# Phase 1 of a metaformer block: x also loaded by channels and scaled there, scatters in two groups of four, xr normalised in two halves

## The chip, the cores and the metric

One core of one Trainium2 chip. The metric is device time in microseconds (us); the kernel before takes 1960.43 us, the median of 3 runs (1958.6 to 1961.08).

## What is computed

The input x is (16, 56, 56, 96) in fp32, 50176 tokens of 96 channels. First a "conv" block: x is normalised over its channels, cut into windows of 7 x 7 and normalised once more (both together are one centring and one scale per token, with a small rescaling of the variance), and a linear recurrence runs over the 49 tokens of each window. Its output `xr` is normalised again and goes through an MLP 96 to 384 to 96. Then a mixture of experts, two of four per token.

```python
w = _ln(_ln_c(x) cut in 7x7 windows, ln1_w, ln1_b)
xs = w @ Bm                          # 49 steps per window
h = xs[t] + h @ A                    # the recurrence
xr = h @ Cm
y = gelu(_ln(xr, ln2_w, ln2_b) @ W1 + b1) @ W2 + b2
x = x + xr + y
t = _ln_t(x); probs = softmax(t @ gate_w + gate_b), two largest kept and rescaled
x = x + sum_e masked[e] * (gelu(t @ w1[e] + b1[e]) @ w2[e] + b2[e])
```

## The kernel before

The work has two phases. Phase 1 runs over 49 tiles; tile t holds the t-th token of all 1024 windows, so that the recurrence goes from tile to tile. A tile is 8 groups of 128 tokens (`SUBS`), tokens on partitions, or 96 channels on partitions by 1024 tokens after a transpose. Each token's row (its sum, its gate scores, its normalised value, its number) is scattered to DRAM, sorted by the pair of experts that it chose. Phase 2 reads the sorted rows in 103 blocks of 512 tokens and runs the experts; the change does not touch it.

The order in phase 1 is written out by hand: every engine has its own loop `for p in periods()`, and semaphores tie the engines. In period p TensorE (PE) does, in this order: the recurrence for tile r = p+1 (`from_state(r)`, L1067, which adds A times the state, then `from_input(r)`, L1074, which adds B times `x_t`) into `mix_ps`; two `up` products of tile p (L1039 to L1041); the rank products of tile p-2 (L1095); `sum_xr(r)` (L1080), which overwrites `mix_ps` with xr by tokens; `down` and `up` in turn (L1048); eight transposes of the normalised x of tile p+2 (L1026, `x_n` to `turn_ps`); `turn_y(p, 0)` (L1056); `down(p, 4)`, `down(p, 5)`; eight transposes of the normalised xr (L1026, `xr_n` to `turn_ps`); `turn_y(p, 1)`. `mix_ps` has one buffer: `from_state(r+1)` waits until xr of tile r has been normalised.

ScalarE (ACT) in period p: `y_hi` from `turn_ps` (L565); four of the eight `normalise_x(p+2)` (L522); `h_t` from `mix_ps` (L572); GELU 0 and 1 (L548); the other four of `normalise_x`; four of `normalise_rows(p-2)` (L539); GELU 2 and 3; `copy_y(p, 0)` (L557); GELU 4; `normalise_xr(r)`, eight instructions (L532); GELU 5; `x_t` from `turn_ps` (L593); `copy_y(p, 1)`.

VectorE (DVE) in period p: `y_lo` (L834); `add_x2(p-1, 1)` (L769); statistics of the sum of tile p-1, of x of tile p+3 and of xr of tile r (L712, L718, L723); `take_xr(r)` (L730 to L736); `shift_of_r` (L742), which waits for GpSimd; `positions(p-2)` (L818 to L828); `add_x2(p, 0)`, which waits for `turn_y(p, 0)`; `shift_of_x(p+3)` (L748, L750); `shift_of_rows`, `gate(p-1)` (L776 to L808); four of `normalise_rows(p-1)` (L760).

GpSimd (POOL) in period p: the inverse deviation of xr (`rstd_of_r`, L423), those of x and of the sum in one instruction (L436), then the eight scatters of tile p-2 (L447). Both are powers of a variance that DVE has written. SyncE (SP) loads x, up to five tiles ahead (L297). The lines on which the change rests:

```python
                if tile(p + 2):                                  # PE
                    turn.take(pe, x_t_ok, p + 3)
                    pe.wait_ge(x_n_ok, p + 3)
                    to_channels(x_n[:, (p + 2) % 2, :, :]).then_inc(x_turned, 1)
...
                if tile(p + 2):                                  # ACT
                    act.wait_ge(x_turned, p + 3)
                    if p + 2 >= 1:
                        act.wait_ge(h_summed, p + 2)
                    act.copy(x_t[0:C, :], turn_ps[0:C, :]).then_inc(x_t_ok, 1)
```

Of the kernel before, what the change touches and what calls it, by code (L numbers as in the profile page):

```python
# [57 lines left out]
X_RING = 5  # L58
DEV_RING = 4
# [17 lines left out]
X_FIRST = 2  # L77
# [8 lines left out]
def periods():  # L86
    return range(-3, TILES + 2)
# [14 lines left out]
def build_program(nc, x, up_w, state_w, turned_w, mlp_down_w, down_w, gate_w, up_b, gate_b, down_b, ln_wb, out):  # L102
# [16 lines left out]
    with ctx:
# [43 lines left out]
        x_n = sb("x_n", [P, 2, SUBS, C])  # L163
# [16 lines left out]
        shift_x = sb("shift_x", [P, 2, SUBS])  # L180
        shift_t = sb("shift_t", [P, HALF_SUBS])
# [111 lines left out]
        def _(sp):  # L293
# [89 lines left out]
        def _(pool):  # L383
# [41 lines left out]
            def rstd_of_x_and_t(t):  # L425
# [6 lines left out]
                if 2 <= t < TILES + 2:  # L432
                    pool.wait_ge(x_n_ok, t - 1)
# [803 lines left out]
```

## Time and profile before

| | us |
|---|---|
| median of 3 runs | 1960.43 |
| the profiled execution | 1960.39 |
| its span, first to last instruction | 1958.7 |
| PE busy over the span | 1871.8 (96%) |
| ACT busy | 1599.1 (82%) |
| DVE busy | 1490.5 (76%) |
| POOL busy | 1355.4 (69%) |

Phase 1 takes the first 950 us or so, 49 tiles at 17.77 us each in its steady part, and phase 2 the rest. Busy matmul time is modelled, since matmuls overlap, so the distance between the starts of PE's rows says more than its busy share: 17.77 us is such a distance, from the first `from_state` row of one period to that of the next.

### The profile page before, as it was taken

The page shows a single profiled execution, that of the slowest core. Times are in us where ns is not written, and L with a number is a line of the kernel's source. Part 1 is how long each engine was busy: PE and PEld are TensorE (multiplying, and loading weights), DVE is VectorE, ACT ScalarE, POOL GpSimd, SP SyncE. Part 2 cuts the span into 40 slices and gives each one's busy share as a digit, 9 for nine tenths or more (in the row PEclk, how much of TensorE's full clock was granted, in tenths as well). Part 3 has the DMA queues.
Part 4 walks back from the last instruction along what each step waited for, and adds up shares of the span by engine and source line. Part 5 has one row for each costly group of instructions (what it writes and reads, how often), then busy time and mean ns, then how long its engine had stood idle before and what let it go on. Part 6 is the DMA issues. An engine that isn't in the chain of part 4 may idle for free.

```text
span 1958.7 us, 36640 instructions
## 1 busy us (share of the span) xinstructions
PE 1871.8 (96%) x8883; PEld 1302.6 (67%) x8883; DVE 1490.5 (76%) x6676; ACT 1599.1 (82%) x3068; POOL 1355.4 (69%) x1097
## 2 busy tenths in 40 slices
PE   5979999999999999997599999999999999999996
PEld 3546666666666666664377777777777777777774
DVE  5767887788777877786477777777777777777775
ACT  3868887888888888875499989999999899999995
POOL 3357767776767677667477777777777777777775
PEclk9989999999999999998699999999999999999998
DMA  4042212222222222111666666666666666666662
GB/s 127 28 114 68 71 67 69 68 71 67 71 67 71 67 70 69 61 51 52 214 211 211 208 207 204 206 206 209 213 208 209 206 202 206 214 210 212 209 208 75
DMA packets 121158, 272.93 MB, mean 139 GB/s; under 512 B 26148, under 2 KB 34749, under 8 KB 120946
## 3 DMA queue, kind: packets, MB, share of 16 engines
q1 hardware_dynamic: 85840, 209.93, 35.6%
q0 software_dynamic: 32000, 58.87, 8.7%
q10 hardware_dynamic: 3106, 1.78, 0.3%
q8 instruction: 74, 1.21, 0.3%
q14 instruction: 138, 1.13, 0.2%
HBM read 204.47 MB, written 66.98 MB: 139 GB/s over the span
## 4 chain that ended last, share of the span: by engine, by line
PE 50%; POOL 27%; issue 20%; DVE 1%; DMA 1%; POOLq 0%; ACTq 0%; ACT 0%; SPq 0%; DVEq 0%
POOL sorted_rows L447 19%; PE mix_ps L1170 7%; PE mix_ps L1171 7%; PE mix_ps L1172 7%; POOL rstd_xt L436 7%; PE turn_ps L1156 4%; PE up_ps L1156 4%; PE turn_ps L1157 4%; PE turn_ps L1158 4%; PE up_ps L1157 4%; PE up_ps L1158 4%; PE tok_ps L1179 3%; PE y_ps L1142 2%; POOL rows L444 1%; POOL rstd_r L423 0%
## 5 line engine op out<-in xcount | busy, mean ns | idle before, releaser
L480 POOL DMA_INDIRECT out<-out_sb,idx x412 | 424.1, 1029 | 262.7 <-DVE out_sb L968 156.2
L924 DVE TENSOR_TENSOR g_lo<-g,g_hi 128x512 fp32r<-128x512 f32 x618 | 423.9, 686 | 198.5 <-ACT g_hi L613 198.5
L447 POOL DMA_INDIRECT sorted_rows<-rows,pos x392 | 383.3, 978 | 118.9 <-issue 104.8
L613 ACT CAST g_hi<-g 128x512 fp32r<-128x512 f32 x618 | 380.8, 616 | 13.1
L1048 PE MATMUL y_ps<-g,d_mlp 128*100 128x512 f32 x588 | 307.2, 604 | 6.5 <-ACT g L548 1.8
L469 POOL TENSOR_TENSOR ex<-euler,rows 128x16 f32<-128x16 f32 x103 | 305.2, 2963 | 10.1 <-DMA rows<-sorted_rows 9.7
L1170 PE MATMUL mix_ps<-g_hi,ew 128*96 128x512 f32 x618 | 244.1, 395 | 0.2 <-DVE g_lo L924 0.2
L1171 PE MATMUL mix_ps<-g_hi,ew 128*96 128x512 f32 x618 | 244.0, 395 | 0.0
L1172 PE MATMUL mix_ps<-g_lo,ew 128*96 128x512 f32 x618 | 243.7, 394 | 0.0
L548 ACT ACTIVATE g<-up_ps 128x512 f32<-128x512 f32 x294 | 172.7, 605 | 60.1 <-PE up_ps L1041 54.9
L423 POOL TENSOR_TENSOR rstd_r<-var_eps,neg_half 128x8 f32<-128x8 f32 x49 | 81.7, 1668 | 193.0 <-DVE var_eps L723 193.0
L607 ACT ACTIVATE g<-turn_ps 128x512 f32<-128x512 f32 x310 | 184.4, 595 | 33.0 <-PE turn_ps L1158 19.4
L607 ACT ACTIVATE g<-up_ps 128x512 f32<-128x512 f32 x308 | 183.4, 595 | 29.4 <-PE up_ps L1158 16.7
L1039 PE MATMUL up_ps<-y_hi,w_hi 98*128 98x512 f32 x294 | 195.0, 663 | 1.8 <-DVE y_lo L834 1.8
L625 ACT ACTIVATE y_sb<-mix_ps,ew 96x512 f32<-96x512 f32 x206 | 140.9, 684 | 23.1 <-PE mix_ps L1172 2.0
L522 ACT ACTIVATE x_n<-x_in,shift_x,rstd_xt 128x96 f32<-128x96 f32 x392 | 150.3, 456 | 8.0 <-DVE shift_x L748 8.0
L436 POOL TENSOR_TENSOR rstd_xt<-var_eps,neg_half 128x16 f32<-128x16 f32 (+1 forms) x53 | 143.5, 2708 | 5.6 <-DVE var_eps L723 5.6
L532 ACT ACTIVATE xr_n<-mix_ps,shift_r,rstd_r 128x96 f32<-128x96 f32 x392 | 131.2, 447 | 17.9 <-DVE shift_r L742 17.8
L1156 PE MATMUL turn_ps<-y_hi,ew 98*128 98x512 f32 x310 | 136.4, 440 | 1.4 <-DVE y_lo L929 1.4
L1156 PE MATMUL up_ps<-y_hi,ew 98*128 98x512 f32 x308 | 134.7, 437 | 0.0
L769 DVE TENSOR_TENSOR rows<-tok_ps,x_xr 128x400 f32<-128x400 f32 x98 | 55.6, 567 | 103.2 <-PE tok_ps L1056 103.2
L1048 PEld LDWEIGHTS y_ps<-g,d_mlp 128*100 128x100 f32 x588 | 86.8, 167 | 65.0 <-ACT g L548 48.2
(181 smaller groups left out, 4164.9 us busy)
## 6 DMA issues: line engine op xcount, KB each, us to landing
ew<-expert_w SPq DMA_DIRECT2D x206, 384.0 KB, 4.2
ew<-expert_w SPq DMA_DIRECT2D x206, 288.5 KB, 3.5
rows<-sorted_rows SPq DMA_DIRECT2D x103, 394.0 KB
x_in<-in_x SPq DMA_DIRECT2D x49, 384.0 KB, 3.1
out<-out_sb,idx POOLq DMA_INDIRECT x412
sorted_rows<-rows,pos POOLq DMA_INDIRECT x392, 2.5
sorted_rows<-pad_rows SPq DMA_DIRECT2D x11, 394.0 KB, 5.0
expert_w<-w_hi SPq DMA_DIRECT2D x4, 192.0 KB, 3.9
```

Of the source, the lines that this page charges most:

```text
L436: pool.tensor_tensor(rstd_xt[:, t % 2, which, :], var_eps[:, 1 + which.start:1 + which.stop, :], neg_half[:, which, :], ALU.pow).then_inc( ...
L447: pool.indirect_dma_start(out=sorted_rows[:, :], out_offset=bass.IndirectOffsetOnAxis(ap=pos[:, r, s:s + 1], axis=0), in_=rows[:, r, s, :] ...
L469: pool.tensor_tensor(ex[:, b % 2, :, :], euler[:, :].rearrange("p (s e) -> p s e", s=BSUBS), rows2[:, b % IN_RING, :, COL_BELOW:COL_T], AL ...
L480: pool.indirect_dma_start(out=out_rows, out_offset=bass.IndirectOffsetOnAxis(ap=idx[:, r, s:s + 1], axis=0), in_=out_sb[:, r, s, :], in_of ...
L607: act.activation(g[:, n % G_RING, :], up_bank(n), ACT.Gelu).then_inc(gelu2_done, 1)
L613: act.copy(g_hi[:, n % PART_RING, :], g[:, n % G_RING, :]).then_inc(hi_done, 1)
L924: dve.tensor_tensor(g_lo[:, n % PART_RING, :], g[:, n % G_RING, :], f(g_hi[:, n % PART_RING, :]), ALU.subtract).then_inc(lo_done, 1)
L1048: pe.matmul(y_ps[0:CG, :], d_mlp[:, k, :], g[:, n % G_RING, :], start=(k == 0), stop=(k == KB - 1)).then_inc(down_done, 1)
L1156: pe.matmul(up_bank(n), hi[0:KR, :], t_hi, start=True, stop=False)
L1170: pe.matmul(y2_bank(q), hi, g_hi[:, part, :], start=(k == 0), stop=False)
L1171: pe.matmul(y2_bank(q), lo, g_hi[:, part, :], start=False, stop=False)
L1172: pe.matmul(y2_bank(q), hi, g_lo[:, part, :], start=False, stop=(k == KB - 1)).then_inc(down2_done, 1)
```

## The change

x is loaded twice: by tokens as before (it still serves the statistics and the residual), and by channels, 96 partitions by 1024 tokens, into `x_raw_t` with two buffers (`load_x_t`). The inverse deviations of x are written to DRAM as a row (`rstd_rows`, 128 partitions by 32 bytes) and read back to 96 partitions, 4 KB to each (`turn_rstd`). DVE multiplies the two (`scale_x`); the row of deviations lies with the 8 groups of one partition side by side, so it is read with a step of 8 elements. The centring goes into the weights (`b_aug`, once). With that the eight `normalise_x`, the eight transposes of x and the copy of `x_t` are gone. All eight `normalise_rows` run on ACT. The second half of a tile's scatters comes one period later, ahead of `rstd_of_r`, behind a wait on `h_summed`. `normalise_xr` is two groups of four with GELU 4 and 5 between them, and the transposes of xr wait for each half. `turn_y(p, 1)` moves behind `from_state` of the next period.

```diff
+            def load_x_t(t):
+                if t >= XT_RING:
+                    sp.wait_ge(x_t_ok, t - XT_RING + 1)
+                sp.dma_start(x_raw_t[:, t % XT_RING, :], x_chan[t, :, :]).then_inc(x_t_loaded[t % XT_RING], 16)
+
+            def turn_rstd(t):
+
+                sp.wait_ge(rstd_xt_ok, t + 1)
+                sp.dma_start(rstd_rows[t, :].rearrange("(p s) -> p s", s=SUBS), rstd_xt[:, t % 2, 0, :]).then_inc(rstd_saved, 16)
+                if t >= 1:
+                    sp.wait_ge(x_t_ok, t)
+                sp.wait_ge(rstd_saved, 16 * (t + 1))
+                sp.dma_start(rstd_t[:, :], rstd_rows[t:t + 1, :].to_broadcast([C, TOK])).then_inc(rstd_t_loaded, 16)
...
+            for t in range(XT_RING, TILES):
+                load_x_t(t)
+                if t + X_RING - XT_RING < TILES:
+                    load_x(t + X_RING - XT_RING)
+                turn_rstd(t)
+                if t == X_RING + 1:
+                    save_experts()
...
                 if 2 <= t < TILES + 2:
-                    pool.wait_ge(x_n_ok, t - 1)
+                    pool.wait_ge(rstd_saved, 16 * (t - 1))
...
             for p in periods():
+                if tile(p - 3):
+                    if tile(p + 1):
+
+                        pool.wait_ge(h_summed, p + 2)
+                    scatter(p - 3, range(HALF_SUBS, SUBS))
                 if tile(p + 1):
                     rstd_of_r(p + 1)
                 if tile(p + 3) or tile(p - 1):
                     rstd_of_x_and_t(p + 3)
                 if tile(p - 2):
-                    scatter(p - 2, range(SUBS))
+                    scatter(p - 2, range(HALF_SUBS))
...
+            def normalise_xr(t, part):
                 if part == 0:
-                    act.wait_ge(shift_x_ok, t + 1)
-                    if t >= 2:
-                        act.wait_ge(x_turned, t - 1)
+                    act.wait_ge(shift_r_ok, t + 1)
+                    if t >= 1:
+                        act.wait_ge(xr_turned, t)
                 for s in range(part * HALF_SUBS, (part + 1) * HALF_SUBS):
...
-                ins.then_inc(xr_n_ok, 1)
+                ins.then_inc(xr_n_ok if part == 1 else xr_half_ok, 1)
...
+            def scale_x(t):
+                i = t % XT_RING
+                dve.wait_ge(x_t_loaded[i], 16 * (t // XT_RING + 1))
+                dve.wait_ge(rstd_t_loaded, 16 * (t + 1))
+                if t >= 1:
+                    dve.wait_ge(h_summed, t)
+                dve.tensor_tensor(x_t[0:C, :].rearrange("c (s p) -> c s p", s=SUBS), x_raw_t[:, i, :].rearrange("c (s p) -> c s p", s=SUBS),
+                                  rstd_t[:, :].rearrange("c (p s) -> c s p", s=SUBS), ALU.mult).then_inc(x_t_ok, 1)
...
                 if tile(p - 2):
                     positions(p - 2)
+                if tile(p + 2):
+                    scale_x(p + 2)
                 if tile(p):
                     add_x2(p, 0)
...
                 if tile(p - 1):
                     shift_of_rows(p - 1)
                     gate(p - 1)
-                    normalise_rows(p - 1)
...
                 if tile(r):
                     from_state(r)
+                if tile(p - 1):
+                    turn_y(p - 1, 1)
+                if tile(r):
                     from_input(r)
...
-                if tile(p + 2):
-                    turn.take(pe, x_t_ok, p + 3)
-                    pe.wait_ge(x_n_ok, p + 3)
-                    to_channels(x_n[:, (p + 2) % 2, :, :]).then_inc(x_turned, 1)
...
                 if tile(r):
                     turn.take(pe, y_lo_ok, r + 1)
+                    pe.wait_ge(xr_half_ok, r + 1)
+                    to_channels(xr_n, 0)
                     pe.wait_ge(xr_n_ok, r + 1)
-                    to_channels(xr_n).then_inc(xr_turned, 1)
-                if tile(p):
-                    turn_y(p, 1)
+                    to_channels(xr_n, 1).then_inc(xr_turned, 1)
```

On PE, from the last `down` ahead of the transposes to the first `up` of the next period, the order was this (a row ends with the semaphores on which it waits):

```order
L1048 MATMUL y_ps<-g,d_mlp 100x512 [waits y_copied,gelu_done]
L1026 MATMUL turn_ps<-ident,x_n 96x128 [waits x_n_ok,y_lo_ok]
L1026 MATMUL turn_ps<-ident,x_n 96x128 x7
L1056 MATMUL tok_ps<-ident,y_sb 128x100 [waits y_copied,base_set]
L1048 MATMUL y_ps<-g,d_mlp 100x512 [waits gelu_done] x2
L1026 MATMUL turn_ps<-ident,xr_n 96x128 [waits xr_n_ok,x_t_ok]
L1026 MATMUL turn_ps<-ident,xr_n 96x128 x7
L1056 MATMUL tok_ps<-ident,y_sb 128x100 [waits y_copied,x2_ok]
L1067 MATMUL mix_ps<-h_t,a_aug 100x512 [waits xr_n_ok,x_xr_ok,h_t_ok]
L1074 MATMUL mix_ps<-x_t,b_aug 100x512 [waits x_t_ok]
```

and is now this:

```order
L1069 MATMUL y_ps<-g,d_mlp 100x512 [waits y_copied,gelu_done]
L1077 MATMUL tok_ps<-ident,y_sb 128x100 [waits y_copied,base_set]
L1069 MATMUL y_ps<-g,d_mlp 100x512 [waits gelu_done] x2
L1047 MATMUL turn_ps<-ident,xr_n 96x128 [waits xr_half_ok,y_lo_ok]
L1047 MATMUL turn_ps<-ident,xr_n 96x128 x3
L1047 MATMUL turn_ps<-ident,xr_n 96x128 [waits xr_n_ok]
L1088 MATMUL mix_ps<-h_t,a_aug 100x512 [waits xr_n_ok,x_xr_ok,h_t_ok]
L1077 MATMUL tok_ps<-ident,y_sb 128x100 [waits y_copied,x2_ok]
L1095 MATMUL mix_ps<-x_t,b_aug 100x512 [waits x_t_ok]
```

The eight transposes of `x_n` are gone, those of `xr_n` have two waits and no longer wait for the copy of `x_t`, and the second `tok_ps` group stands behind `from_state` (L1088).

On DVE the middle of a period, between `positions` and `gate`, read

```order
L828 CAST pos<-place_sum 128x8
L769 TENSOR_TENSOR rows<-tok_ps,x_xr 128x4x100
L748 SCALAR_TENSOR_TENSOR shift_x<-moment,rstd_xt 128x8
L750 TENSOR_TENSOR dev_x<-var_eps,rstd_xt 128x8
L755 SCALAR_TENSOR_TENSOR shift_t<-moment,rstd_xt 128x4
```

and reads

```order
L846 CAST pos<-place_sum 128x8
L778 TENSOR_TENSOR x_t<-x_raw_t,rstd_t 96x1024
L787 TENSOR_TENSOR rows<-tok_ps,x_xr 128x4x100
L764 TENSOR_TENSOR dev_x<-var_eps,rstd_xt 128x8
L769 SCALAR_TENSOR_TENSOR shift_t<-moment,rstd_xt 128x8
```

`scale_x` (L778) stands ahead of `add_x2(p, 0)`, `shift_x` is gone. On POOL one period is now

```order
L475 DMA sorted_rows<-rows,pos 306688x197 [waits h_summed]
L475 DMA sorted_rows<-rows,pos 306688x197 x3
L451 TENSOR_TENSOR rstd_r<-var_eps,neg_half 128x8 [waits xr_n_ok,var_ok0]
L464 TENSOR_TENSOR rstd_xt<-var_eps,neg_half 128x16 [waits rstd_saved,t_n_ok,var_ok2,var_ok1]
L472 TENSOR_SCALAR rows<-ids 128x8 [waits t_n_ok,pos_step]
L475 DMA sorted_rows<-rows,pos 306688x197 [waits id_ok]
L475 DMA sorted_rows<-rows,pos 306688x197 x3
```

where eight scatters in one run stood behind L444 before.

## Rows read from the trace of the kernel before

**Rows 1.** Busy by stretch: PE, PEld, DVE, ACT, POOL; PEclk, DMA share, GB/s

```profile
300.00:500.00 200.00, 198.71 (x900) 122.70 (x900) 162.16 (x980) 162.44 (x349) 141.36 (x126) 1.00 0.21 69
...
950.00:1958.00 1008.00, 986.55 (x4944) 755.58 (x4944) 767.90 (x2369) 888.65 (x1545) 729.09 (x515) 0.99 0.66 202
```

**Rows 2.** Timeline of PE, one period: start, us, operation, count

```profile
409.07 1.88 PE L1067 MATMUL mix_ps<-h_t,a_aug 96*100 96x512 f32 x4
410.79 1.88 PE L1074 MATMUL mix_ps<-x_t,b_aug 97*100 97x512 f32 x4
...
422.15 1.03 PE L1026 MATMUL turn_ps<-ident,x_n 128*96 128x128 f32 x8
423.02 0.51 PE L1056 MATMUL tok_ps<-ident,y_sb 100*128 100x100 f32 x4
...
425.44 1.04 PE L1026 MATMUL turn_ps<-ident,xr_n 128*96 128x128 f32 x8
426.47 0.54 PE L1056 MATMUL tok_ps<-ident,y_sb 100*128 100x100 f32 x4
426.84 1.45 PE L1067 MATMUL mix_ps<-h_t,a_aug 96*100 96x512 f32 x3
```

**Rows 3.** Timeline of PE's weight loads: idle before, releaser

```profile
424.50 0.25 PEld L1048 LDWEIGHTS y_ps<-g,d_mlp 128*100 128x100 f32 x2 [0.96 <-ACT g L548]
425.36 0.86 PEld L1026 LDWEIGHTS turn_ps<-ident,xr_n 128*96 128x96 f32 x8 [0.61 <-ACT x_t L593]
```

**Rows 4.** Timeline of ACT, the same period

```profile
421.28 2.67 ACT L532 ACTIVATE xr_n<-mix_ps,shift_r,rstd_r 128x96 f32<-128x96 f32 x8
423.80 0.64 ACT L548 ACTIVATE g<-up_ps 128x512 f32<-128x512 f32 x1
```

**Rows 5.** Timeline of DVE, the same period

```profile
420.20 0.19 DVE L742 SCALAR_TENSOR_TENSOR shift_r<-moment,rstd_r 128x8 f32<-128x8 f32 x1 [0.74 <-POOL rstd_r L423]
...
423.57 0.58 DVE L769 TENSOR_TENSOR rows<-tok_ps,x_xr 128x400 f32<-128x400 f32 x1 [2.07 <-PE tok_ps L1056]
...
426.77 1.02 DVE L760 TENSOR_SCALAR rows<-rows,moment,rstd_xt 128x96 f32<-128x96 f32 x4
427.71 1.21 DVE L834 TENSOR_TENSOR y_lo<-turn_ps,y_hi 96x1024 fp32r<-96x1024 f32 x1
```

**Rows 6.** Groups of DVE by form, 100 to 850 us: busy us, mean ns

```profile
L794 DVE TENSOR_REDUCE rank<-beaten 128x32 f32<-128x128 f32 x41 | 11.7, 286 | 1.4
...
L826 DVE TENSOR_REDUCE place_sum<-place 128x8 f32<-128x48 f32 x42 | 10.2, 243 | 1.5
L801 DVE TENSOR_TENSOR of_pair<-kept 128x24 f32<-128x24 f32 x41 | 8.9, 218 | 1.4
```

**Rows 7.** Timeline of POOL, the same period

```profile
418.49 1.67 POOL L423 TENSOR_TENSOR rstd_r<-var_eps,neg_half 128x8 f32<-128x8 f32 x1 [2.83 <-DVE var_eps L723]
420.15 2.89 POOL L436 TENSOR_TENSOR rstd_xt<-var_eps,neg_half 128x16 f32<-128x16 f32 x1
...
425.00 0.96 POOL L447 DMA_INDIRECT sorted_rows<-rows,pos  x1 [0.30 <-issue]
```

**Rows 8.** Timeline of DVE while POOL's L436 runs

```profile
420.81 0.21 DVE L824 TENSOR_TENSOR place<-place,of_pair 128x48 f32<-128x48 f32 x1
421.05 0.24 DVE L826 TENSOR_REDUCE place_sum<-place 128x8 f32<-128x48 f32 x1
```

**Rows 9.** DMA issues, 100 to 850 us: KB each, median us to landing

```profile
x_in<-in_x SPq DMA_DIRECT2D x43, 384.0 KB, 3.1
sorted_rows<-rows,pos POOLq DMA_INDIRECT x332, 2.5
```

**Rows 10.** Timeline of POOL: the first and the last of 49 L423, the last L436

```profile
32.14 1.64 POOL L423 TENSOR_TENSOR rstd_r<-var_eps,neg_half 128x8 f32<-128x8 f32 x1 [14.53 <-DVE var_eps L723]
...
898.11 1.67 POOL L423 TENSOR_TENSOR rstd_r<-var_eps,neg_half 128x8 f32<-128x8 f32 x1 [3.97 <-DVE var_eps L723]
...
925.44 1.67 POOL L436 TENSOR_TENSOR rstd_xt<-var_eps,neg_half 128x8 f32<-128x8 f32 x1 [1.25 <-DVE var_eps L723]
```

More of the change, by code:

```diff
@@ L58 @@
 X_RING = 5
+XT_RING = 2
 DEV_RING = 4
@@ L76 @@
 FIRST_LOADS, GATE_LOADS, MLP_LOADS, LATER_LOADS = 4, 4, 3, 2
-X_FIRST = 2
 GATE_SUMS = 4
@@ L86, in periods @@
 def periods():
-    return range(-3, TILES + 2)
+    return range(-3, TILES + 3)
 class Region:
@@ L162, in build_program @@
         x_in = sb("x_in", [P, X_RING, SUBS, C])
-        x_n = sb("x_n", [P, 2, SUBS, C])
+        x_raw_t = sb("x_raw_t", [C, XT_RING, TOK])
+        rstd_t = sb("rstd_t", [C, TOK])
         x_t = sb("x_t", [C + 1, TOK])
@@ L231, in build_program @@
         x_loaded = [sem(f"x_loaded{i}") for i in range(X_RING)]
+        x_t_loaded = [sem(f"x_t_loaded{i}") for i in range(XT_RING)]
+        rstd_saved, rstd_t_loaded = sem("rstd_saved"), sem("rstd_t_loaded")
         const_step = sem("const_step")
@@ L307, in _ @@
             sp.dma_start(f(w_hi[C + 1:KR, 0:HID]), f(b_lo[:, 0:HID])).then_inc(bias_rows, 16)
-            for t in range(X_FIRST, X_RING):
+            for t in range(XT_RING, X_RING):
                 load_x(t)
+            turn_rstd(1)
             sp.wait_ge(const_step, CONSTS)
@@ L575, in _ @@
                     gelu(p, 1)
-                if tile(p + 2):
-                    normalise_x(p + 2, 1)
                 if tile(p - 2):
@@ L583, in _ @@
                     copy_y(p, 0)
+                if tile(r):
+                    normalise_xr(r, 0)
+                if tile(p):
                     gelu(p, 4)
+                    gelu(p, 5)
                 if tile(r):
-                    normalise_xr(r)
-                if tile(p):
-                    gelu(p, 5)
-                if tile(p + 2):
-                    act.wait_ge(x_turned, p + 3)
-                    if p + 2 >= 1:
-                        act.wait_ge(h_summed, p + 2)
-                    act.copy(x_t[0:C, :], turn_ps[0:C, :]).then_inc(x_t_ok, 1)
+                    normalise_xr(r, 1)
                 if tile(p):
@@ L1022, in gate_products, with to_channels @@
                           start=True, stop=True).then_inc(gate_sums, 1)
-            def to_channels(src):
-                for s in range(SUBS):
+            def to_channels(src, h):
+                for s in range(HALF_SUBS * h, HALF_SUBS * (h + 1)):
                     ins = pe.transpose(turn_ps[0:C, sub(s)], src[:, s, :], ident[:, :])
@@ L1086, in _ @@
                     from_state(r)
+                if tile(p - 1):
+                    turn_y(p - 1, 1)
+                if tile(r):
                     from_input(r)
```

92 lines of the change are left out of this document (39 added, 53 removed).

## The prediction

> **What bounds the kernel now.** I read the busy times by stretch first. Between 300 and 500 us PE is busy for 198.7 of 200 us, DVE and ACT for 162, POOL for 141, at the full clock; the 1008 us behind 950 us are phase 2, which the change leaves alone [rows 1]. So only the length of a period in phase 1 can move, and a little at its two ends. The timeline of PE gives that length: from `from_state` at 409.07 to the next at 426.84 us, 17.77 us [rows 2]. Then the waits inside it. Eight transposes of x_n take 423.02 - 422.15 = 0.87 us. From the start of `turn_y` at 423.02 to the transposes of xr at 425.44 us lie 2.42 us, which hold four half-products of 0.43 us (four of the same kind take 410.79 - 409.07 = 1.72 us) and `turn_y`, 0.35 us: 0.35 us is left over [rows 2]. It is the wait for GELU 5 [rows 3], which ACT can start only at 423.80 us, behind eight `normalise_xr` from 421.28 us on [rows 4]. The transposes of xr take 426.47 - 425.44 = 1.03 us, 0.16 more than those of x_n [rows 2], since they wait for the copy of `x_t` [rows 3]. PE therefore loses 0.5 us of a period to ACT and is otherwise the bound.
>
> The other engines have room. In 17.77 us DVE stands idle for 0.74 us ahead of `shift_r` (it waits for the power on POOL) and 2.07 us ahead of `add_x2(p, 0)` (it waits for `turn_y`) [rows 5]. POOL stands idle for 2.83 us ahead of L423 [rows 7].
>
> **The change, part by part.**
>
> *PE.* Eight transposes go: -0.87. The waits for GELU 5 and for `x_t` go: -0.5. `turn_y(p, 1)` only moves, by 0.35 us to the other side of `from_state`: 0. In ACT's new order GELU 4 stands behind four `normalise_xr` instead of behind none. These last half of 2.67 us [rows 4], and PE arrives at `down(p, 4)` 0.87 us sooner; laid out from `from_state`, PE is there at 13.8 us and GELU 4 is done at 13.95 us: about +0.2. PE's own period would be 17.77 - 0.87 - 0.5 + 0.2 = 16.6 us. The two waits in place of one ahead of the transposes of xr cost nothing: the first half has been normalised 2 us before PE arrives, the second half at about the moment when the first four transposes end.
>
> *ACT.* It loses eight `normalise_x` and the 96x1024 copy, and gains four `normalise_rows`. It had room before; cost nothing.
>
> *DVE.* This is the crux. Taken out: the four `normalise_rows`, 427.71 - 426.77 = 0.94 us, and `shift_x`, 0.07 us. Put in: `scale_x`, ahead of `add_x2(p, 0)`, in the 2.07 us for which DVE stood idle there [rows 5]. If it fills them, the period of DVE is 17.77 - 2.07 - 0.94 - 0.07 + s = 14.7 + s, with s the time of `scale_x`; the 0.74 us ahead of `shift_r` stay, as they come from POOL's power behind the statistics of xr. No row has `scale_x`. The nearest in size is `y_lo`, 96x1024 in order: 1.21 us [rows 5]. With L794 (128 elements, 286 ns [rows 6]) this gives (1210 - 286) / 896 = 1.03 ns for an element, and 48 elements should take 286 - 80 x 1.03 = 204 ns. But L826, which reads its 48 elements with a step of 8, 32 bytes, as `scale_x` reads `rstd_t`, takes 243 ns [rows 6]: 39 ns more for 8 runs of 6, that is for 40 steps inside a run, 1.0 ns a step. `scale_x` has 8 x 127 = 1016 such steps, so s = 1.21 + 1.02 = 2.2 us. Bounds: 1.21 us, if steps cost nothing in a product; and L801, which *writes* 24 elements with this step, takes 218 where 286 - 104 x 1.03 = 179 would be due [rows 6], 1.6 ns an element, so 1.21 + 1.7 = 2.9 us. I take 2.2, from the only row that reads this way. The period of DVE is then 14.7 + 2.2 = 16.9 us.
>
> The Trainium skill ("SBUF — State Buffer", the note on cachelines) says that SBUF has lines of 16 bytes and that accesses which leave the line each time pay a penalty; it gives no size. By it a product in order would be the exception and 1.21 us out of reach; the row of L826 agrees.
>
> *POOL.* The work stays the same: 1.66 us and 2.89 us of powers, eight scatters at 0.96 + 0.30 us each, and with the numbers of the tokens 17.77 - 2.83 = 14.9 us together [rows 7]. New is where they wait. The second four start when `from_input` is done, about 3.7 us after `from_state`, and end at 8.8 us; the variance of xr is ready at 418.49 - 409.07 = 9.4 us [rows 2, 7] and about 0.4 us later in the new order. The first four end 3.1 us into the next period, ahead of `h_summed`. Both have slack (1.0 and 0.6 us), so L423, which is queued behind the second four, and with it `shift_r` and `normalise_xr`, are not held up: 0. Landing takes 2.5 us [rows 9], until 11.3 us, and `add_x2(p, 0)`, which reuses those rows, comes after 14 us.
>
> *SP and the DMA.* Per tile one more load of 384 KB, a write of 4 KB, and a broadcast of 384 KB. The deviations are there at about 14.3 us of a period. The row that I have for such a transfer is 3.1 us [rows 9]; with two in a row, one waiting for the other, the broadcast lands near 21 us, and `scale_x` wants it at 16.9 + 12.8 = 29.7 us: 8 us of slack. Bandwidth goes from 69 GB/s to some 115, where phase 2 runs at 202 [rows 1]. SP waits in the middle of a tile for the write to land, behind which are the next loads; those are one to three periods early. Nothing.
>
> **The sum.** The period is the longer of 16.6 (PE) and 16.9 (DVE): 16.9, a gain of 0.87 us. It counts between the first and the last L423, 48 periods; the whole stretch is 898.11 - 32.14 = 866 us [rows 10], and as its first two periods are not yet full, I count 46: 40 us. Behind the last L423 POOL has four tiles to scatter with only 1.25 us of idle time [rows 10], before and after: 0. Ahead of the first, the transposes and the copy of tile 0 and 1 go, and `scale_x` waits for a write and a broadcast instead; I put both and the first two periods at -3 us (anything from +3 to -5). From the profiled execution's 1960.39 us: 1960.4 - 43 = 1917 us. The median is 1960.43, so it needs no correction.
>
> **The rivals.**
>
> *PE stays the bound.* If the steps cost nothing, DVE needs 14.7 + 1.21 = 15.9 us and the period is PE's 16.6: 1.17 x 46 + 3 = 57, 1903 us; without the 0.2 us at GELU 4, 1894 us. For: no row has a two-input product with steps. Against: L826, and L801 too. 0.2.
>
> *The steps cost more.* With s = 2.9 us the period is 17.6, the gain 0.17 x 46 + 3 = 11, 1949 us; from s = 3.1 on nothing is left of it but the start. 0.13 for more than 2.5 us, of which 0.05 within 4 us of no change.
>
> *Slower: `scale_x` waits for POOL's power.* It reads two tensors in SBUF, and stands ready at about the moment (421.4 us in the timeline before) when L436 has started; that runs from 420.15 to 423.04 us [rows 7]. If the one shuts out the other, `scale_x` starts 1.6 us late, the period is 16.9 + 1.6 = 18.5, and 46 x 0.73 - 3 = 31 us are lost: 1991 us. It decides as soon as DVE is held for over 0.9 us. Against it: L824 reads two tensors in SBUF, from 420.81 us on, in the middle of that same L436, and takes 0.21 us [rows 8], where 204 ns is what its 48 elements need. 0.07.
>
> The Trainium skill ("SBUF — State Buffer", on the shared port pair) states this as a rule: a DVE operation with two SBUF inputs and a GpSimd operation that reads SBUF take the pair for the whole instruction, and the other blocks. By it the case above would be the rule; the trace does not agree, at L824's size.
>
> *The scatters or the chain through DRAM come late.* If the second four end over 1 us later, every further 0.1 us is 0.1 us of each period. If it were 1.5 us, the period is 17.4 and the time 1940. Against: each scatter shows the same 0.96 us. 0.05, in the range.
>
> **How the numbers follow.** A measurement of this kernel can tell 0.2% (4 us) from no change. My forecast, DVE as the bound at 16.6 to 17.2 us, has 0.55; PE as the bound 0.2; dear steps 0.13; late scatters 0.05; the slower case 0.07. Faster: 0.55 + 0.2 + 0.08 + 0.04 = 0.87; within 0.2%: 0.05; slower: 0.08. The range leaves out the slower case and the far ends of two others: 1894 to 1946 us.
>
> **What would show it.** Right: no `x_n` on PE, `scale_x` at 2.0 to 2.4 us each, 49 of them, no idle time ahead of `add_x2(p, 0)`, a distance of 16.9 us between `from_state` rows, and PE waiting 0.2 to 0.4 us a period for `y_lo` or GELU 4; L423 still waits for L723, and the scatters stay at 0.96 us. Wrong: `scale_x` at 1.2 us or above 2.6 us; `scale_x` or L423 waiting for a DMA or for scatters; L423 preceded by a scatter without a gap; a start to the first `up` that is more than 3 us later than before.

## The result and the profile after

| | median, us | range of the runs | ratio to before, 95% interval |
|---|---|---|---|
| before | 1960.28 | 1958.6 to 1961.08 | |
| changed | 1887.24 | 1887.15 to 1887.43 | 0.9629 (0.9612 to 0.9645) |

The change saves 73 us, 3.7%. The forecast was 1917 us with a range of 1894 to 1946: right sign, but the time lies 7 us below the range. The changed kernel's profiled execution has a span of 1885.4 us against 1958.7. One thing lies outside all these times: x by channels is a second input (`x_chan`), laid out in numpy before the device program starts, just as the cut of x into windows was already.

Its page, with the busy time of each engine over the span:

```profile
PE 1810.8 (96%) x8493; PEld 1266.1 (67%) x8493; DVE 1531.8 (81%) x6481; ACT 1482.8 (79%) x2823; POOL 1367.8 (73%) x1097
```

PE's share has not moved from 96% although it lost 61 us of work, and DVE has gone from 76% to 81%. The same by stretch, in the columns of [rows 1]:

```profile
300.00:500.00 200.00, 200.00 (x872) 123.98 (x871) 183.77 (x998) 145.49 (x318) 155.20 (x134) 1.00 0.41 121
...
876.00:1885.00 1009.00, 985.61 (x4944) 756.88 (x4944) 767.40 (x2369) 890.25 (x1545) 728.82 (x515) 0.99 0.66 202
```

In phase 1 PE is busy for all of the 200 us (before 198.7), DVE for 183.8 where it was 162.2, and the traffic is 121 GB/s, close to the 115 of the forecast. Phase 2 takes 1009 us, where it took 1008. The timeline of PE over one period of the changed kernel, which answers to [rows 2]:

```profile
402.46 1.88 PE L1088 MATMUL mix_ps<-h_t,a_aug 96*100 96x512 f32 x4
404.18 0.51 PE L1077 MATMUL tok_ps<-ident,y_sb 100*128 100x100 f32 x4
404.53 1.88 PE L1095 MATMUL mix_ps<-x_t,b_aug 97*100 97x512 f32 x4
...
415.87 0.51 PE L1077 MATMUL tok_ps<-ident,y_sb 100*128 100x100 f32 x4
416.33 1.96 PE L1069 MATMUL y_ps<-g,d_mlp 128*100 128x512 f32 x4
418.13 1.04 PE L1047 MATMUL turn_ps<-ident,xr_n 128*96 128x128 f32 x8
419.00 1.45 PE L1088 MATMUL mix_ps<-h_t,a_aug 96*100 96x512 f32 x3
```

The period is 419.00 - 402.46 = 16.54 us, down from 17.77. From `turn_y` at 415.87 to the transposes of xr at 418.13 us are 2.26 us, of which 0.35 and 4 x 0.43 are work: the wait for the GELUs has shrunk from 0.35 to 0.19 us. The transposes of xr take 0.87 us, where they took 1.03 before. DVE in the same period, answering to [rows 5]:

```profile
413.94 0.19 DVE L760 SCALAR_TENSOR_TENSOR shift_r<-moment,rstd_r 128x8 f32<-128x8 f32 x1 [0.74 <-POOL rstd_r L451]
...
415.20 2.03 DVE L778 TENSOR_TENSOR x_t<-x_raw_t,rstd_t 96x1024 f32<-96x1024 f32 x1
417.15 0.56 DVE L787 TENSOR_TENSOR rows<-tok_ps,x_xr 128x400 f32<-128x400 f32 x1
```

`scale_x` takes 2.03 us, not 2.2 (2.01 to 2.04 over 44 of them). The 2.07 us of idle time ahead of `add_x2(p, 0)` are gone, and the 0.74 us ahead of `shift_r` are as they were. POOL, answering to [rows 7]:

```profile
406.69 0.95 POOL L475 DMA_INDIRECT sorted_rows<-rows,pos  x1 [0.80 <-PE mix_ps L1095]
...
412.24 1.67 POOL L451 TENSOR_TENSOR rstd_r<-var_eps,neg_half 128x8 f32<-128x8 f32 x1 [0.81 <-DVE var_eps L741]
413.89 2.89 POOL L464 TENSOR_TENSOR rstd_xt<-var_eps,neg_half 128x16 f32<-128x16 f32 x1
416.87 0.43 POOL L472 TENSOR_SCALAR rows<-ids 128x8 f32<-128x8 f32 x1
```

The second four scatters wait 0.80 us for `from_input`, and L451 still waits for the variance, not for scatters. These waits sum to 1.61 us where L423 waited for 2.83; no DMA holds anything here.

**Where the 73.3 us of the two spans lie.** The 49 rows of the power of xr (L423 before, L451 now) are milestones. The first stands at 32.14 us before [rows 10] and at 30.00 now, the sixth at 134.26 and 114.52, the last at 898.11 and 825.74:

| stretch | before, us | changed, us | gain | in the forecast |
|---|---|---|---|---|
| start to the first | 32.14 | 30.00 | 2.1 | 3 |
| first to sixth | 102.12 | 84.52 | 17.6 | 2.6 |
| sixth to last, 43 periods | 763.85 | 711.22 | 52.6 (1.22 each) | 37.4 (0.87 each) |
| last to the end | 1060.6 | 1059.7 | 0.9 | 0 |
| sum | 1958.7 | 1885.4 | 73.2 | 43 |

Two lines carry what was missed, 30 us: the periods are shorter by 0.35 us more than forecast (15 us), and the first five gain 15 us too much. Of the latter, most is one wait of DVE in the kernel before, 11.0 us long:

```profile
111.33 1.38 DVE L712 BATCH_NORM_STATS2 stats<-x_in 128x6 f32<-128x96 f32 x8 [11.01 <-DMA x_in<-in_x]
```

Why that load came late stands in SP's queue of the kernel before (the first and last rows of the experts' weights, L326, with the loads of x around them), and in the list of its waits from 30 to 160 us (in total, times, longest):

```profile
39.50 0.58 SPq L297 DMA_DIRECT2D x_in<-in_x  x1
92.94 0.34 SPq L326 DMA_DIRECT2D expert_w<-w_hi  x1
...
104.11 0.46 SPq L326 DMA_DIRECT2D expert_w<-b_col  x1
104.61 12.58 SPq L297 DMA_DIRECT2D x_in<-in_x  x4
```

```profile
SPq L326 <- DVE d_lo L708: 52.2, 1, 52.2
```

SP issued one x tile at 39.50 us, then stood for 52.2 us at the wait for the last experts' weights. The next loads of x were queued behind the twenty writes of `save_experts` and went out at 104.61 us. The change puts `save_experts` behind four more loads (`if t == X_RING + 1: save_experts()` in the loop with `load_x(t + 3)`), and the wait is gone.

### The profile page after: what moved, and what is told of

It reads as the page before. It is cut to its first block, busy times and chain, and to the rows that moved or that the text cites. A ratio compares the mean times of both kernels' runs of the same rounds, so it can differ in the third digit from the quotient of the medians.

```text
span 1885.4 us, 35473 instructions
## 1 busy us (share of the span) xinstructions
PE 1810.8 (96%) x8493; PEld 1266.1 (67%) x8493; DVE 1531.8 (81%) x6481; ACT 1482.8 (79%) x2823; POOL 1367.8 (73%) x1097
## 4 chain that ended last, share of the span: by engine, by line
PE 52%; POOL 29%; issue 16%; DMA 1%; DVE 1%; POOLq 0%; ACTq 0%; ACT 0%; SPq 0%; DVEq 0%
POOL sorted_rows L475 20%; PE mix_ps L1190 8%; PE mix_ps L1192 8%; PE mix_ps L1191 8%; POOL rstd_xt L464 7%; PE up_ps L1176 4%; PE turn_ps L1176 4%; PE turn_ps L1177 4%; PE up_ps L1177 4%; PE turn_ps L1178 4%; PE up_ps L1178 4%; PE tok_ps L1199 4%; PE y_ps L1162 2%; POOL rows L472 1%; DMA rows<-in_up_b 0%
## 5 line engine op out<-in xcount | busy, mean ns | idle before, releaser
L1069 PE MATMUL y_ps<-g,d_mlp 128*100 128x512 f32 x588 | 297.5, 600 | 2.2 <-ACT g L571 2.2
L571 ACT ACTIVATE g<-up_ps 128x512 f32<-128x512 f32 x294 | 166.5, 605 | 59.1 <-PE up_ps L1062 54.9
L623 ACT ACTIVATE g<-up_ps 128x512 f32<-128x512 f32 x308 | 183.5, 596 | 29.5 <-PE up_ps L1178 16.8
L593 ACT COPY h_t<-mix_ps 100x1024 f32<-100x1024 f32 x49 | 49.6, 1012 | 148.7 <-PE mix_ps L1095 148.7
L464 POOL TENSOR_TENSOR rstd_xt<-var_eps,neg_half 128x16 f32<-128x16 f32 (+1 forms) x53 | 143.3, 2703 | 6.2 <-DVE var_eps L741 6.2
L562 ACT ACTIVATE rows<-rows,shift_t,rstd_xt 128x96 f32<-128x96 f32 x392 | 145.1, 455 | 3.2 <-DVE shift_t L769 3.2
L555 ACT ACTIVATE xr_n<-mix_ps,shift_r,rstd_r 128x96 f32<-128x96 f32 x392 | 138.4, 455 | 8.4 <-DVE shift_r L760 8.4
L451 POOL TENSOR_TENSOR rstd_r<-var_eps,neg_half 128x8 f32<-128x8 f32 x49 | 81.7, 1667 | 85.8 <-DVE var_eps L741 85.8
L1191 PEld LDWEIGHTS mix_ps<-g_hi,ew 128*96 128x96 f32 x618 | 101.0, 163 | 43.4
```

The lines of the kernel that those rows point to most:

```text
L464: pool.tensor_tensor(rstd_xt[:, t % 2, which, :], var_eps[:, 1 + which.start:1 + which.stop, :], neg_half[:, which, :], ALU.pow).then_inc( ...
L623: act.activation(g[:, n % G_RING, :], up_bank(n), ACT.Gelu).then_inc(gelu2_done, 1)
L1069: pe.matmul(y_ps[0:CG, :], d_mlp[:, k, :], g[:, n % G_RING, :], start=(k == 0), stop=(k == KB - 1)).then_inc(down_done, 1)
L1191: pe.matmul(y2_bank(q), lo, g_hi[:, part, :], start=False, stop=False)
```

## The experiments

All ran beside the kernel before on the same chip, and the ratios are to that: its medians were 1956.77 us beside runs 1, 2, 4 and 5, 1956.48 beside 3, 6, 8 and the first kernel of 7, and 1957.38 beside the rest. It was some 3 us faster there than beside the changed kernel, so differences of 1 us from 1887.24 say nothing, and the period decides. A period is the distance between two `from_state` rows near 400 us. "Run 4" is the kernel under number 4.

**1. The kernel before, with `save_experts` later.** Its loads of x are issued first, as in the change, and nothing else is touched.

```diff
-            load_x(X_RING)
-            sp.wait_ge(later_prep, 4)
...
-            for t in range(X_RING + 1, TILES):
+            for t in range(X_RING, TILES):
                 load_x(t)
+                if t == X_RING + 4:
+                    save_experts()
```

> The kernel before with one thing changed: SP saves the expert weights behind the load of x of tile 9 instead of ahead of that of tile 6. Theory (queue): the kernel before had one period of 29.0 us instead of 17.8 (distance of two L423 rows, 86.86 to 115.87 us), with DVE waiting 11.0 us for a load of x, because that load stood in SP's queue behind the wait for the last expert weights. Then all periods are 17.8 us and the time is 11 us shorter, 1949 us. Rival (bandwidth): the load was late because the saved weights filled the DMA engines; then the stall only moves to a later tile and the time stays at 1958 to 1961.

Measured: 1947.03 us, ratio 0.9948 (0.9932 to 0.9965), so 10 us of the 73 have nothing to do with x by channels. DVE no longer waits for a DMA from 60 to 160 us, and the milestones there follow at the steady distance, where the kernel before has one distance of 115.87 - 86.86 = 29.0 us:

```profile
86.53 1.64 POOL L426 TENSOR_TENSOR rstd_r<-var_eps,neg_half 128x8 f32<-128x8 f32 x1 [13.69 <-DVE var_eps L726]
104.34 1.67 POOL L426 TENSOR_TENSOR rstd_r<-var_eps,neg_half 128x8 f32<-128x8 f32 x1 [1.81 <-DVE var_eps L726]
...
121.25 1.67 POOL L426 TENSOR_TENSOR rstd_r<-var_eps,neg_half 128x8 f32<-128x8 f32 x1 [1.85 <-DVE var_eps L726]
```

The first milestone stands at 32.12 us and the sixth at 121.25, so the first five distances take 89.1 us, 13.0 less than before.

**2. The changed kernel, with the deviations read in order.** This is the rival of the forecast with s = 1.21 us. x is then scaled by the deviations of other tokens, which changes the output but no other instruction.

```diff
-                dve.tensor_tensor(x_t[0:C, :].rearrange("c (s p) -> c s p", s=SUBS), x_raw_t[:, i, :].rearrange("c (s p) -> c s p", s=SUBS),
-                                  rstd_t[:, :].rearrange("c (p s) -> c s p", s=SUBS), ALU.mult).then_inc(x_t_ok, 1)
+                dve.tensor_tensor(x_t[0:C, :], x_raw_t[:, i, :], rstd_t[:, :], ALU.mult).then_inc(x_t_ok, 1)
```

> The changed kernel, but scale_x reads the row of deviations in order, so that x is scaled by the deviations of other tokens; the work is the same but for the step. Theory (PE bound): scale_x falls from 2.03 to 1.2 us, the period stays at 16.54 us, the time within 3 us of 1887. Rival (DVE bound, the forecast's): the period falls by up to 0.8 us, to 1850.

Measured: 1886.06 us, 0.9635 (0.9619 to 0.9651); `scale_x` takes 1.22 us, and the period stays at 16.54 us. DVE gives its 0.8 us back as idle time:

```profile
405.45 1.22 DVE L851 TENSOR_TENSOR y_lo<-turn_ps,y_hi 96x1024 fp32r<-96x1024 f32 x1 [0.71 <-ACT y_hi L588]
```

The steps cost time on DVE and none of the kernel's: DVE is not the bound.

**3. The product with other steps.** Tiles 7 to 13, and so on in turn, read `rstd_t` with a step of 1, 2, 4, 8, 16 and 32 elements, or write with a step of 8. Here too x is scaled by wrong deviations.

```diff
+                kind, n = (("in", 1), ("in", 2), ("in", 4), ("in", 8), ("in", 16), ("in", 32), ("out", 8))[t % 7]
...
+                dve.tensor_tensor(dst(x_t[0:C, :], n), flat_view(x_raw_t[:, i, :], n), src(rstd_t[:, :], n), ALU.mult).then_inc(x_t_ok, 1)
```

> The changed kernel, with scale_x of tile t reading the row of deviations with a step of 1, 2, 4, 8, 16, 32 elements for t mod 7 = 0 to 5, and for t mod 7 = 6 reading it in order and writing x_t with a step of 8 (so x is scaled by wrong deviations). It prices the step. The forecast's reading of L826 (1.0 ns for each step inside a run) gives 1.21 us at step 1, 2.2 us at 8, 2.2 at 16 and 32; measured at 8 so far is 2.03. If SBUF lines of 16 bytes decide, steps of 1 to 2 cost 1.2 us, 4 lies at the edge, and 8 and more cost the same 2.0 us. If the distance in bytes matters, 16 and 32 cost more than 8. Writing with a step of 8: 2.0 us if writes pay like reads, 2.9 us by the rate of L801.

Measured, in DVE's timeline, for steps of 1, 2, 4, 8, 16 and 32, and last for the write with a step of 8:

```profile
135.06 1.22 DVE L786 TENSOR_TENSOR x_t<-x_raw_t,rstd_t 96x1024 f32<-96x1024 f32 x1
151.60 1.22 DVE L786 TENSOR_TENSOR x_t<-x_raw_t,rstd_t 96x1024 f32<-96x1024 f32 x1
168.13 2.03 DVE L786 TENSOR_TENSOR x_t<-x_raw_t,rstd_t 96x1024 f32<-96x1024 f32 x1
184.68 2.02 DVE L786 TENSOR_TENSOR x_t<-x_raw_t,rstd_t 96x1024 f32<-96x1024 f32 x1
201.21 1.92 DVE L786 TENSOR_TENSOR x_t<-x_raw_t,rstd_t 96x1024 f32<-96x1024 f32 x1
217.76 1.96 DVE L786 TENSOR_TENSOR x_t<-x_raw_t,rstd_t 96x1024 f32<-96x1024 f32 x1
234.30 2.03 DVE L786 TENSOR_TENSOR x_t<-x_raw_t,rstd_t 96x1024 f32<-96x1024 f32 x1
```

The price is (2.03 - 1.22) / 1016 = 0.8 ns for each step; it is there in full at 16 and 32 bytes, absent at 8 bytes, a little less at 64 and 128 bytes, and the same for the one write. The whole kernel ran once, in 1886.38 us.

**4. `scale_x` twice.** A second product of the same size goes into a scratch buffer that phase 1 doesn't use.

```diff
+                dve.tensor_tensor(out_sb[0:C, :, :, :].rearrange('p a s c -> p (a s c)')[:, 0:TOK].rearrange("c (s p) -> c s p", s=SUBS), x_raw_t[:, i, :].rearrange("c (s p) -> c s p", s=SUBS),
+                                  rstd_t[:, :].rearrange("c (p s) -> c s p", s=SUBS), ALU.mult)
```

> The changed kernel with scale_x done twice, once into a buffer that phase 1 does not use. DVE has 1.95 us more in a period. If DVE has no slack at all in 16.54 us, the period is 18.5 us and the time 1887 + 49 x 1.95 = 1983 us. If DVE has 0.5 us of slack it is 18.0 and 1960. The trace shows DVE waiting for y_hi by almost nothing, so I expect 18.4 to 18.5.

Measured: 1970.78 us, 1.0071 (1.0054 to 1.0088), and a period of 18.34 us, with PE's weight loads waiting for `y_lo`:

```profile
PEld up_ps L1062 <- DVE y_lo L854: 34.1, 22, 1.6
```

Here DVE is the bound, and its own period can be read from start to start:

```profile
406.88 0.56 DVE L789 TENSOR_TENSOR rows<-tok_ps,x_xr 128x400 f32<-128x400 f32 x1
...
421.33 2.01 DVE L778 TENSOR_TENSOR out_sb<-x_raw_t,rstd_t 96x1024 f32<-96x1024 f32 x1
423.25 2.02 DVE L780 TENSOR_TENSOR x_t<-x_raw_t,rstd_t 96x1024 f32<-96x1024 f32 x1
425.20 0.56 DVE L789 TENSOR_TENSOR rows<-tok_ps,x_xr 128x400 f32<-128x400 f32 x1
```

425.20 - 406.88 = 18.32 us hold two products; one adds 1.92 to 1.95 us, so by this run the changed kernel's DVE needs 16.4 us of its 16.54, and the bound is PE, by 0.14 us. Run 9 makes this 0.2 us: there DVE goes round in 16.34. Part of the difference is that some small instructions of the gate take longer here (L821 with 128x16 elements takes 237 ns, and 179 in run 9).

**5. More work for PE.** Eight transposes of a constant stand ahead of those of xr, into columns that these overwrite.

```diff
+                    for s in range(SUBS):
+                        pe.transpose(turn_ps[0:C, sub(s)], earlier[:, 0:C], ident[:, :])
```

> The changed kernel with eight more transposes of a constant into turn_ps ahead of those of xr in each period (they do nothing for the result). PE has 0.87 us more in a period. Theory (PE bound): the period is 17.4 us, the time 1887 + 48 x 0.87 = 1929 us. Rival (DVE bound, PE with slack): less than that; with DVE as the only bound the period stays at 16.54.

Measured: 1926.54 us, 0.9842 (0.9826 to 0.9859), period 17.40 us. Of the 0.87 us that the transposes take, 0.86 reach the period. With run 2 this settles it: 0.8 us less on DVE change nothing, 0.87 us more on PE count in full.

**6. The scatters in one group again.**

```diff
-                if tile(p - 3):
-                    if tile(p + 1):
-
-                        pool.wait_ge(h_summed, p + 2)
-                    scatter(p - 3, range(HALF_SUBS, SUBS))
...
-                    scatter(p - 2, range(HALF_SUBS))
+                    scatter(p - 2, range(SUBS))
```

> The changed kernel with all eight scatters of a tile in one run behind L472, as before, and no wait on h_summed. POOL's work is 14.9 us of 16.54, and the eight end 8.3 us into the next period, where the variance of xr comes at 9.6. Theory: the two groups are worth nothing by themselves, the period stays 16.54 us and the time within 3 us of 1887. Rival: the eight end late for L451, each 0.1 us of it is paid in each period; at 17.0 us the time is 1910.

Measured: 1886.38 us, 0.9639 (0.9623 to 0.9655), period 16.54 us, and L451 waits for 1.25 us in one piece. Two groups are worth nothing in this kernel; POOL has the room either way.

**7. `normalise_xr` whole, and halves alone.** In the changed kernel ACT's order goes back to GELU 4, eight `normalise_xr`, GELU 5:

```diff
+                if tile(p):
+                    gelu(p, 4)
                 if tile(r):
                     normalise_xr(r, 0)
-                if tile(p):
-                    gelu(p, 4)
-                    gelu(p, 5)
-                if tile(r):
                     normalise_xr(r, 1)
                 if tile(p):
+                    gelu(p, 5)
```

> The changed kernel with normalise_xr in one piece of eight between GELU 4 and GELU 5, as before. PE then waits for GELU 5 ahead of down(p, 5), as it did before the change, by 0.35 us or, since it arrives 0.87 us sooner without the transposes of x, by up to 1.2 us. I expect a period of 17.3 to 17.6 us and 1925 to 1940 us: the removed transposes alone bring little, the halves bring the rest. Rival: the wait is covered, and the period stays below 16.7 us.

Measured: 1932.4 us, 0.9873 (0.9857 to 0.989), period 17.56 us. PE stands still ahead of its last `down`:

```profile
422.45 1.10 PE L1068 MATMUL y_ps<-g,d_mlp 128*100 128x512 f32 x2 [0.99 <-ACT g L571]
```

and ACT's timeline says why: GELU 5 starts at 421.76 us, behind the eight.

```profile
419.23 2.69 ACT L555 ACTIVATE xr_n<-mix_ps,shift_r,rstd_r 128x96 f32<-128x96 f32 x8
421.76 0.64 ACT L571 ACTIVATE g<-up_ps 128x512 f32<-128x512 f32 x1
```

The counterpart: the kernel before with nothing but the halves. ACT's order is GELU 4, four `normalise_xr`, GELU 5, the copy of `x_t`, the other four.

```diff
-                    normalise_xr(r)
+                    normalise_xr(r, 0)
...
+                if tile(r):
+                    normalise_xr(r, 1)
...
+                    pe.wait_ge(xr_half_ok, r + 1)
+                    to_channels(xr_n, range(HALF_SUBS))
                     pe.wait_ge(xr_n_ok, r + 1)
-                    to_channels(xr_n).then_inc(xr_turned, 1)
+                    to_channels(xr_n, range(HALF_SUBS, SUBS)).then_inc(xr_turned, 1)
```

> The kernel before (with its transposes of x) with one part of the change: normalise_xr in two halves, the second behind GELU 5 and the copy of x_t, and the transposes of xr waiting for each half. In the changed kernel, undoing the halves cost 1.03 us a period. If they are worth something without the removal of the transposes of x, PE loses its wait for GELU 5 (0.35 us a period), but may wait 0.1 to 0.3 us for the second half, which stands behind the copy: 17.4 to 17.7 us a period, 1941 to 1957 us beside 1957. If the two parts only work together, the period stays at 17.77.

Measured: 1943.76 us, 0.9924 (0.9909 to 0.9939), period 17.54 us. The four corners are 17.77 (before), 17.54 (halves alone), 17.56 (everything else) and 16.54 us (all). Alone the two parts bring 0.23 and 0.21 us, together 1.23. With the transposes gone but `normalise_xr` whole, PE only arrives sooner at the same late GELU. With the halves alone the 0.35 us of waiting for GELU 5 are gone, but PE waits elsewhere:

```profile
418.75 1.13 PE L1030 MATMUL turn_ps<-ident,xr_n 128*96 128x128 f32 x8
419.91 0.53 PE L1060 MATMUL tok_ps<-ident,y_sb 100*128 100x100 f32 x4
```

From the transposes to `turn_y` are 1.16 us (before 1.03), as `copy_y` stands behind the second half on ACT and ends at 419.76. 0.35 less 0.13 are the 0.23 us measured. "Everything else" also holds the move of `turn_y`, which run 8 prices at 0.19 us, so what the two parts bring only together is not all due to halves and transposes.

**8. `turn_y(p, 1)` back behind the transposes.**

```diff
-                if tile(p - 1):
-                    turn_y(p - 1, 1)
...
+                if tile(p):
+                    turn_y(p, 1)
```

> The changed kernel with turn_y(p, 1) behind the transposes of xr, as before. copy_y(p, 1) ends at 419.02 us in the trace of the changed kernel, where the transposes of xr end at 419.0: PE would wait some 0.1 us for it, and otherwise nothing changes. I expect 16.54 to 16.7 us a period, 1887 to 1895 us. Rival: the move is worth the whole length of copy_y, 0.5 us a period, 1911 us.

Measured: 1895.28 us, 0.9683 (0.9667 to 0.9699), period 16.73 us. From the transposes at 407.76 us to `turn_y` are 1.03 us again, not 0.87, although no copy of `x_t` is left to wait for. What ends then is the copy of the output, on ACT:

```profile
407.97 0.69 ACT L580 ACTIVATE y_sb<-y_ps,b_col 100x512 f32<-100x512 f32 x1 [0.27 <-PE y_ps L1069]
```

It ends at 408.66 us, and `turn_y`, which reads it, starts at 408.80, 0.14 us later. The same distance stands in the kernel before, where `copy_y` ends at 426.33 us and `turn_y` starts at 426.47 [rows 2]:

```profile
425.64 0.69 ACT L557 ACTIVATE y_sb<-y_ps,b_col 100x512 f32<-100x512 f32 x1 [0.33 <-PE y_ps L1048]
```

The 0.16 us were `turn_y`'s wait for `copy_y`, and the move, which the forecast put at 0, is worth 0.19 us a period, 8 us in all.

**9. GELU 4 first, and the same with an earlier start.** The first takes the last wait out of PE's period:

```diff
+                if tile(p):
+                    gelu(p, 4)
...
-                    gelu(p, 4)
```

> The changed kernel with GELU 4 ahead of the first half of normalise_xr. PE waits 0.1 us a period for GELU 4 now. The first half is needed only at the transposes of xr, 2 us later. PE bound: 16.43 us a period and 1882 us. Rival: DVE, whose slack in 16.54 us came out as 0.15 us with scale_x done twice, or y_hi behind the second half, gives it back: no change.

Measured: 1876.86 us, 0.9586 (0.9573 to 0.96), period 16.34 us, 0.09 below what was expected. PE goes on without a gap: `down` starts 0.34 us behind `turn_y`, and 1.72 us later the transposes. The second variant also moves the load by channels of tile 1 behind the row of deviations of tile 0.

```diff
-            for t in range(XT_RING):
-                load_x(t)
-                load_x_t(t)
+            load_x(0)
+            load_x_t(0)
+            load_x(1)
...
+            load_x_t(1)
```

> The kernel of a9_gelu4_first, with the load by channels of tile 1 moved behind the row of deviations of tile 0. In the changed kernel the first weights land 3 us later than before (PE starts at 9.4 us, not 6.1) and scale_x of tile 0 waits until 18.5 us for the deviations through DRAM. With 384 KB less ahead of them, the first scale_x starts 1 to 3 us sooner, and so does everything behind it: 1880 us. Rival: the start hangs on something else, and the time is that of a9_gelu4_first.

Measured: 1875.81 us, 0.9582 (0.9569 to 0.9595), which can't be told from the first, as the rival of the expectation had it; the first `scale_x` starts at 18.25 us instead of 18.46. Both beat the changed kernel by some 10 us. At 16.34 us DVE has no slack left. In the first variant `y_lo` no longer waits for anything, it starts while the row ahead of it ends:

```profile
417.88 0.26 DVE L827 TENSOR_TENSOR_SCAN count<-restart,of_pair 128x48 fp32r<-128x48 f32 x1
418.05 1.20 DVE L853 TENSOR_TENSOR y_lo<-turn_ps,y_hi 96x1024 fp32r<-96x1024 f32 x1
```

The `y_lo` before it starts at 401.74 us, 16.31 us earlier. PE's weight loads show first waits for `y_lo`, 7.0 us in 25 of them between 300 and 700 us, while the changed kernel's 16.54 us less its 0.19 of waits for GELUs are 16.35. Both engines end at the same length; which of them holds the other is not shown.

**10. Four `normalise_rows` back on DVE.**

```diff
-                for s in range(SUBS):
+                for s in range(HALF_SUBS, SUBS):
...
+            def normalise_rows(t):                           # DVE
+                for s in range(HALF_SUBS):
...
                     gate(p - 1)
+                    normalise_rows(p - 1)
```

> The changed kernel with four of the eight normalise_rows on DVE, as before. DVE gets 0.94 us more in a period with 0.15 us of slack: 17.3 us a period, 1887 + 48 x 0.8 = 1925 us. Rival: ACT is freed by 1.5 us and PE by nothing, and DVE's new work lies in its wait for y_hi: below 16.7 us, 1890.

Measured: 1920.67 us, 0.9809 (0.9794 to 0.9824), period 17.28 us. 17.28 - 0.94 = 16.34 us: a third reading of DVE's own period, the same as in run 9. Without this move the changed kernel would lose 33 of its 73 us.

## Why the prediction was right and wrong

**PE's period: right.** Forecast 16.6, measured 16.54. The 0.2 us charged to GELU 4 are there: 0.11 us ahead of `down(p, 4)` and 0.08 us inside the four half-products (1.80 for 1.72), and taking them out (run 9) brings 0.20. The 0.5 us of waits were the right amount with one wrong name. The 0.16 were not the copy of `x_t` but `copy_y` (run 8). That this part of the sum came out right is luck: the change also moves `turn_y`, which the forecast put at 0 and which is what removes the wait.

**DVE's period: the step that failed.** It was "14.7 + 2.2 = 16.9"; the runs show 16.34 (runs 9 and 10) to 16.40 (run 4), of which `scale_x` has 1.95 and the rest 14.4. Both terms were too large, by 0.25 and by about 0.3 us:
- s. The price of a step came from 40 steps in one small instruction, a reduction, against a straight line through others, and was 1.0 ns. It is 0.8 (run 3), and the end of `scale_x` overlaps the start of the next instruction by 0.08 us, which start-to-start distances count and durations don't.
- The rest of DVE. I took 17.77 minus the idle time that the trace lists. In the kernel before, from `y_lo` to `positions`' last cast are 421.33 - 409.91 = 11.42 us; in run 4, where DVE is the bound, 421.22 - 409.98 = 11.24, and in run 9 as much. The trace puts no idle time there, yet the statistics of xr start 0.22 us behind the variance ahead of them where 0.08 is enough; 0.14 us of it is slack. The last cast ahead of the listed idle time counts with its whole 0.17 us, where the next row can start 0.11 us behind its start. And about 0.1 us are small instructions of the gate that took longer in the kernel before: L801 with 128x16 elements took 214 ns, and takes 179 (as L819) in the changed kernel. Why is open.

The same L801 gave the bound of 1.6 ns for a write with steps. With 128x24 elements it takes 202 ns in the changed kernel, not 218, so part of that bound was no step at all.

With 16.34 to 16.40 against 16.54 us the order turned over, and what happened is the first rival, PE as the bound, which had 0.2. It came about in another way than the rival said: not because steps are free, but with their full price of 0.8 us a period paid out of slack. 0.35 us over 43 periods are 15 us. This alone doesn't explain the miss, since that rival's own time, 1903 us, is 16 us too long as well.

**The count of periods: the second step that failed.** "As its first two periods are not yet full, I count 46": I took the 866 us between the first and the last L423 and 48 periods, which is 18.04 us each, beside a steady 17.77, and did not ask where 48 x 0.27 = 13 us had gone. Most of it was one wait of 11.0 us, and the diff had the line that removes it. Of SP the forecast said only what is loaded and how early in the steady part. Run 1 prices this part at 10 us by the medians, and at 13.0 of the 17.6 us gained between the first and the sixth milestone. The other 4.6 us are five periods that gain 0.9 each, where the forecast left two of them out and had 2.6 us. At the start the change gave 2.1 us, not 3.

**The other terms.** The rival of dear steps fell with s = 1.95. The slower case did not happen: `scale_x` starts at 415.20 us, in the middle of L464 (413.89 to 416.78), and takes 2.03 us, while L464 keeps its 2.89. In run 4 the second product starts behind the end of L464 (at 423.25 us, after 422.94) and takes 2.02. The rule of the Trainium skill ("SBUF — State Buffer", on the shared port pair) that stood beside this case does not hold for this pair; for others see the last section. Late scatters and the chain through DRAM cost nothing in the steady part, and going back to one group of scatters (run 6) gains and loses nothing. "ACT: cost nothing" held for its work and hid the main point, that its order is worth 1.02 us a period (run 7).

## What to carry to other kernels

When two engines end within 2% of each other, take the period of the one that isn't the bound from start-to-start distances of its rows, not from the period less the listed idle time. Divide the length of the whole stretch by the number of periods: if the mean is above the steady period, look for a single long wait; here it was a load queued behind a semaphore wait. A wait between engines and the work ahead of it can be worth little one at a time and much together, so price them as a pair.

## What the runs showed of the hardware that was not expected

**The price of a step has an edge.** A product of two fp32 tensors in SBUF takes 1.22 us for 1024 elements at steps of 1 and 2, and 2.03 at steps of 4 and of 8 (run 3): no slope, an edge between 8 and 16 bytes. The Trainium skill ("SBUF — State Buffer", the note on cachelines) says that two accesses in each line of 16 bytes are needed for full speed; the edge agrees, since a step of 2 still leaves two fp32 elements in a line and a step of 4 one. It adds that 4 fp32 are how far one can stride for free, with which the 2.03 us at a step of 4 don't agree if a step of 4 is meant. The size, which it doesn't give, is 0.8 ns a step here.

**DVE holds up GpSimd, in short operations.** L472, a `tensor_scalar` of 128x8, took 0.20 us in the kernel before (as L444, 22 of them at 202 ns) and takes 0.47 us now (25 of them at 466 ns): in the period above it starts at 416.87, inside `scale_x`, and ends at 417.30, just behind the end of `scale_x` at 417.23. In run 2, where the product ends at 418.14 us, it starts behind that and takes 0.20 us again:

```profile
418.60 0.20 POOL L472 TENSOR_SCALAR rows<-ids 128x8 f32<-128x8 f32 x1
```

In run 4 it is a scatter, while the second product runs from 423.25 to 425.27 us:

```profile
423.70 2.54 POOL L475 DMA_INDIRECT sorted_rows<-rows,pos  x1 [0.29 <-POOL rows L472]
426.55 0.96 POOL L475 DMA_INDIRECT sorted_rows<-rows,pos  x1 [0.30 <-issue]
```

It ends at 426.24 us, 0.97 us behind the product, which is its usual 0.96: it seems not to have begun until the product was done. So it looks as if this product of two inputs on DVE shuts out a short GpSimd operation and a scatter that start inside it, while the power that was already running went on beside it, and DVE started inside the power without a delay. In this kernel POOL has the slack for it. The Trainium skill ("SBUF — State Buffer", on the shared port pair) lets whichever of the two starts first shut out the other for the whole instruction: the trace agrees where DVE was first and does not where GpSimd was. What decides it was not tried.
